# Graph diffusion by the powers S, S^2 and S^3, and the pivots of the eigenvectors written out row by row

## The chip, the cores and the metric

The kernel runs on one core of one Trainium2 chip. The metric is the device time of one execution, in microseconds (us), as the median of several runs. TensorE multiplies matrices, VectorE and ScalarE work elementwise, and each engine runs its own stream of instructions; they meet only through semaphores.

## The reference, cut to what matters

x is 16 batches of 512 nodes by 128 features, adj is 512 x 512. Four graph layers follow each other, each with a residual sum and a layer norm. The change touches the second, a diffusion of eight Euler steps:

```python
h = jnp.einsum('bnd,ed->bne', x, fc_in_w) + fc_in_b
alph = jax.nn.sigmoid(alpha_train)[:, None]
w_eff = w * jnp.clip(d, 0.0, 1.0) @ w.T
def euler_step(h, _):
    ax = jnp.einsum('nm,bmd->bnd', adj_mx, h)
    f = alph * 0.5 * (ax - h) + h @ w_eff - h + x0
    return (h + dt * f, None)
h, _ = jax.lax.scan(euler_step, h, None, length=8)
```

The third layer needs the eigenvectors U of the normalized Laplacian of adj: `_, U = jnp.linalg.eigh(L_norm)`.

## The kernel before

`build` calls one block after another: Laplacian, tridiagonal form, eigenvalues (by sweeps of the characteristic polynomials), the first layer (`graph_conv`, `lstms`), a layer norm, `turn_x`, `diffusion_terms`, and then the block that is changed, `vectors_and_diffusion`. `back_transform` and the last two layers follow. Between blocks all engines wait for each other.

`diffusion_terms` has turned the eight steps into a polynomial. The result is the sum over i from 0 to 8 of S^i x M_i plus a bias, where S (`k.S`, 512 x 512) holds adj, alpha and the step, M_i (`k.M`, nine of 128 x 128) holds the weights, and r_i (`k.r`, nine rows) the biases. `k.h` holds x turned (features on partitions), `k.x` holds x itself.

In `vectors_and_diffusion` three engines work side by side.

TensorE and ScalarE evaluate the polynomial by Horner's rule. First the bias, in nine rounds of four groups of 128 columns: lines 999 and 1002, each round after ScalarE's copies of the round before (line 1050). Then two halves of eight batches. In a half, for i from 8 down to 0, there are eight groups (two times four batches, by four blocks `nt` of 128 nodes), each in one PSUM bank of 512 columns. A group is four products of `acc` with S (line 1016, 512 columns each; none for i = 8), in the last step one with the identity that adds the bias (line 1020), and four products, one a batch, of turned x with M_i (line 1023, 128 columns each). ScalarE copies each bank to the other half of `acc`, and at last to `k.x` (line 1044). The steps from 6 to 1 stand in a loop of the engines (`Fori`).

VectorE meanwhile finds the eigenvectors of the tridiagonal matrix from its eigenvalues. It runs pivots from both ends (`way` 0 and 1): for each of 511 rows two reciprocals (line 1086) and two multiply-adds (line 1088), 128 x 4 elements each. The helper `Link` with `lag=1` lets an instruction wait for the last but one. The loop has seven rows in its body, with the row's addresses in registers, and ends with a flush and a clear of the semaphore. Then come reciprocals, scans and the squared norms (lines 1098 to 1131). ScalarE takes the root of the norms (line 1060) at a fixed place in its own order, ahead of the last but one round of copies of the second half, and VectorE goes on (line 1134 and after) to fix signs and scale `k.vec`.

The next block, `back_transform`, begins with transposes (line 1232) and needs `k.vec` and all three engines to have finished.

## Time and profile before

| | us |
|---|---|
| median of 3 runs | 5985.85 (5984.94 to 5997.67) |
| the profiled execution | 5985.78 |
| its span | 5984.1 |
| TensorE busy with matmuls | 3705.1 (62% of the span) |
| VectorE busy | 4382.6 (73%) |
| ScalarE busy | 1216.2 (20%) |
| mean granted clock of TensorE | 0.648 of 2.4 GHz |

The span runs from the first to the last instruction. Shares of the whole say little here, because the blocks have different limits: what counts for the change is the stretch from 4642 to 5322 us, in which `vectors_and_diffusion` runs. Idle time of an engine that doesn't set the end of its block costs nothing. A matmul's duration in a row includes a part in which the next one already runs, so a rate has to be read from starts.

### The profile page before, as it was taken

Reading aid. Unit: us, or ns where it says so; the run is one execution under the profiler, and the core shown is the slowest. Engines: PE = TensorE matmul, PEld = TensorE weight load, DVE = VectorE, ACT = ScalarE, POOL = GpSimd, SP = SyncE. Lnnn points to the kernel's source line nnn. Section 1 sums busy time; section 2 is a strip of 40 time slices with the busy share of each in tenths; the row PEclk is TensorE's granted clock in tenths of the full one; section 3 lists DMA queues with packets and bytes.
Section 4 is the critical chain, followed back from the end, with each engine's and each line's share of the span. In section 5 each row is a group of like instructions: output and inputs, shape, how many; then the busy total and the mean of one; then the engine's idle time right before and its main releaser. Section 6 shows DMA issues by size and latency. Waiting matters only on the chain. (4 is left out here: it accounts for less than half of the span.)

```text
span 5984.1 us, 79152 instructions
## 1 busy us (share of the span) xinstructions
PE 3705.1 (62%) x22240; PEld 2430.9 (41%) x22240; DVE 4382.6 (73%) x24246; ACT 1216.2 (20%) x3608; POOL 16.8 (0%) x30
## 2 busy tenths in 40 slices
PE   5666655555555666532333333497894999986674
PEld 4565655555555565500000000142432755553352
DVE  7888988888888877799999999612225777534457
ACT  1222122221222222221222222114321111101000
POOL 0000000000000000000000000000000000000000
PEclk9755555555555555555555555698896699988876
DMA  1000000000000000000000000000000000000001
GB/s 36 2 2 2 2 1 1 1 1 1 1 1 1 1 1 1 1 0 0 0 0 0 0 0 0 22 0 0 0 0 0 1 0 0 0 0 0 0 0 28
DMA packets 14086, 17.02 MB, mean 3 GB/s; under 512 B 624, under 2 KB 10000, under 8 KB 13712
## 3 DMA queue, kind: packets, MB, share of 16 engines
q1 hardware_dynamic: 10896, 9.44, 0.6%
q8 instruction: 157, 2.57, 0.2%
q10 hardware_dynamic: 2352, 2.69, 0.2%
q14 instruction: 217, 1.78, 0.1%
q0 software_dynamic: 464, 0.55, 0.0%
HBM read 8.47 MB, written 4.19 MB: 2 GB/s over the span
## 5 line engine op out<-in xcount | busy, mean ns | idle before, releaser
L805 DVE SCALAR_TENSOR_TENSOR poly<-poly,off,term 128x60 f32<-128x60 f32 x2560 | 608.2, 273 | 0.0
L797 DVE SCALAR_TENSOR_TENSOR term<-cut,rows,poly 128x60 f32<-128x60 f32 x2560 | 596.6, 274 | 11.2 <-DVE poly L816 2.0
L728 PE MATMUL both_signs<-signs,identb 128*128 128x480 bf16 x320 | 186.3, 582 | 569.8 <-PEq L65 569.8
L567 PE MATMUL totals<-pp_sum,ones 128*128 128x2 f32 x768 | 225.3, 363 | 410.6 <-DVE pp_sum L401 410.6
L1016 PE MATMUL horner_ps<-horner,S 128*128 128x512 f32 x1024 | 460.6, 592 | 0.0
L517 PE MATMUL row_e<-vwv 128*128 128x2 f32 (+30 forms) x988 | 301.8, 396 | 217.3 <-DVE x_parts L426 217.3
L528 PEld LDWEIGHTS product<-x_parts,A_parts 128*128 128x128 bf16 x11136 | 405.4, 111 | 42.6 <-DVE A_parts L339 42.6
L528 PE MATMUL product<-x_parts,A_parts 128*128 128x3 bf16 x11136 | 359.9, 167 | 41.6 <-DVE A_parts L339 41.6
L567 PEld LDWEIGHTS totals<-pp_sum,ones 128*128 128x128 f32 x768 | 192.3, 311 | 449.6 <-DVE pp_sum L401 449.6
L1536 PE MATMUL gate_ps<-h_sb,wih_t 128*128 x504 | 317.1, 789 | 81.7 <-PEq L65 81.7
L517 PEld LDWEIGHTS row_e<-vwv 128*128 128x128 f32 x988 | 258.6, 322 | 231.4 <-issue 231.4
L728 PEld LDWEIGHTS both_signs<-signs,identb 128*128 128x128 bf16 x320 | 40.5, 127 | 739.3 <-issue 739.3
L705 ACT ACTIVATE signs<-poly 128x1080 bf16<-128x1080 f32 x160 | 176.5, 1103 | 636.9 <-ACTq L65 636.9
L734 PE MATMUL total<-agree,identb 128*128 128x480 bf16 x320 | 153.4, 583 | 237.4 <-PEq L65 237.4
L618 ACT ACTIVATE vwv<-v,sc 128x8 f32<-128x8 f32 (+3 forms) x510 | 152.3, 299 | 652.5 <-DVE sc L384 627.3
L503 PE MATMUL change<-vwv 128*128 128x2 f32 x764 | 195.3, 348 | 117.9 <-DVE sc L432 117.4
L1016 PEld LDWEIGHTS horner_ps<-horner,S 128*128 128x128 f32 x1024 | 184.8, 190 | 183.6 <-issue 183.6
L1088 DVE SCALAR_TENSOR_TENSOR piv<-rec,sq,piv 128x4 f32 x1022 | 205.7, 223 | 64.9 <-DVE rec L1086 0.4
L512 PE MATMUL coef<-x_on_pairs_sum,ones 128*128 128x2 f32 (+30 forms) x744 | 233.5, 405 | 26.6 <-DVE x_on_pairs_sum L457 20.9
L503 PEld LDWEIGHTS change<-vwv 128*128 128x128 f32 x764 | 182.9, 319 | 133.2 <-issue 132.5
L709 ACT ACTIVATE agree<-both_signs 128x960 bf16<-128x960 f32 x160 | 155.4, 971 | 338.6 <-ACTq L65 338.6
L1536 PEld LDWEIGHTS gate_ps<-h_sb,wih_t 128*128 128x128 f32 x504 | 112.2, 227 | 265.6 <-issue 263.1
(483 smaller groups left out, 7933.1 us busy)
## 6 DMA issues: line engine op xcount, KB each, us to landing
out_dram<-x_sb SPq DMA_DIRECT2D x4, 1024.0 KB, 7.3
adj_sb<-adj_dram SPq DMA_DIRECT2D x1, 1024.0 KB, 6.0
alpha<-L_gnn_alpha_train_dram POOLq DMA_DIRECT2D x1, 256.0 KB, 5.7
edge_row<-L_gnn_src_dram POOLq DMA_DIRECT2D x1, 128.0 KB, 5.5
edge_row<-L_gnn_dst_dram POOLq DMA_DIRECT2D x1, 128.0 KB, 6.0
w<-L_gnn_Wg_dram ACTq DMA_DIRECT2D x2, 64.0 KB, 4.3
w<-L_gnn_W_dram ACTq DMA_DIRECT2D x2, 64.0 KB, 3.8
x_sb<-x_dram SPq DMA_DIRECT2D x4, 0.5 KB, 10.4
```

What stands on the lines that cost most here:

```text
L503: last = pe.matmul(norm_of(n), vwv[:, c, j % 2, 1:2].broadcast_to([P, P]), vwv[:, c, j % 2, 1:3], start=(c == c0), stop=(c == C - 1))
L512: pe.matmul(coef[:, 0:2 * j], k.ones[:], on_pairs_sum[:, 0:2 * j], start=True, stop=True)\
L517: pe.matmul(row_e[:, 0:2 * j].rearrange("p (j t) -> p j t", t=2), vwv[:, c, j % 2, 2:3].broadcast_to([P, P]), vwv[:, c, 2:2 + j, 1:3], sta ...
L528: last = pe.matmul(product[:, r, 0:PARTS], parts[:, i, c, r * P:(r + 1) * P], x_parts[:, c, :], start=(c == c0 and i == 0), stop=(c == C - ...
L567: pe.matmul(totals[:, 0:2], k.ones[:], pp_sum[:], start=True, stop=True).then_inc(dot_ready, 1)
L705: act.activation(sign[:, b], poly[:, b, :, 1:BLOCK + 2, :], ACT.Sign).then_inc(sign_full, 1)
L728: pe.matmul(here, identb[:], rows_of(b, way, 0), start=True, stop=False)
L797: pair(dve.scalar_tensor_tensor(out=term[:, way, :], in0=flat, scalar=rows[:, way, row:row + 1], in1=poly[:, b, way, s + 1, :], op0=ALU.su ...
L805: pair(dve.scalar_tensor_tensor(out=poly[:, b, way, s + 2, :], in0=poly[:, b, way, s, :], scalar=off2[:, way, row:row + 1], in1=term[:, wa ...
L1016: pe.matmul(here, k.S[:, c, nt * P:(nt + 1) * P], acc[:, src, c, j // C * 4:j // C * 4 + 4, :].rearrange("p b d -> p (b d)"), start=(c == ...
L1088: pair(dve.scalar_tensor_tensor(out=pivots(way, 1), in0=rec[:, way, :], scalar=sq[:, ds(i * per + (j + 1), 1), way], in1=pivots(way, 1), o ...
L1536: last = pe.matmul(bank[:, slot, g, 0:n].rearrange("p (b w) -> p b w", w=nw), k.wih_t[:, w + g, :], windows(s, nb, nw, i, slot, t), start= ...
```

## The change

The polynomial is evaluated by Horner's rule in S^3: with g = 2, 1, 0, the sum over g of S^(3g) (x M_3g + S x M_3g+1 + S^2 x M_3g+2).

- S is transposed (`turn`), and S^2 and S^3 are made by products (`square`, `cube`). S^2 lies in `k.u_t`.
- For every batch turned x is multiplied by S and by S^2 (`once`, `twice`) into `moved`.
- A group then takes twelve small products with M (four batches by three) and, for g = 1 and 0, four with S^3. Four batches are done at a time (q = 0 to 3), with g = 2, 1, 0 in turn. Intermediate values lie in `k.x` and `acc`.
- The bias takes three terms in place of nine rounds, with the row sums of S and S^2 (`sum`) for the powers.
- The order of all groups is the list `ORDER`, which is written out for TensorE and ScalarE; banks are taken in turn, group n in bank n % 8. `needed` and two waits inside a group say which copies must be done. ScalarE takes the root ahead of its copy of group (3, 1, 0).
- On VectorE the 511 rows of pivots are written out with fixed addresses, without the loop, its flushes and its clears. `sq` moves into the storage of `k.vec`.

The diff, without most of the removed lines:

```diff
@@ -958,14 +958,17 @@
 
     with ExitStack() as ctx:
         sb, ps, sem = allocators(nc, ctx)
-        acc = sb("horner", [P, 2, C, 8, D])
+        S2, S3 = k.u_t, sb("S3", [P, C, N])
+        moved = sb("moved_x", [P, 2, 4, N])
+        acc = sb("horner", [P, C, 4, D])
+        S_rows = acc[:].rearrange("p c b d -> p c (b d)")
         bias = sb("horner_bias", [P, 2, C, D])
+        sums = sb("sums_of_rows", [1, 2, N])
         bank = ps("horner_ps", [P, 8, N])
         full = sem("horner_full")
         free = sem("horner_free")
-        bias_used = sem("horner_bias_used")
         piv = sb("piv", [P, N, 2, C])
-        sq = sb("sq", [P, N, 2])
+        sq = k.vec[:, 0:2, :].rearrange("p c (n t) -> p (c n) t", t=2)
...
+        ORDER = [("turn", c) for c in range(C)] + [("once", b) for b in range(4)]
+        ORDER += [("square", c) for c in range(C)] + [("twice", b) for b in range(4)]
+        ORDER += [("cube", c) for c in range(C)] + [("sum", j) for j in range(2)] + [("bias", g) for g in (2, 1)]
+        for q in range(B // 4):
+            if q:
+                ORDER += [(power, q * 4 + b) for b in range(4) for power in ("once", "twice")]
+            for g in (2, 1, 0):
+                ORDER += [(q, g, nt) for nt in range(C)]
+                if (q, g) == (0, 2):
+                    ORDER.append(("bias", 0))
+        place = {step: n for n, step in enumerate(ORDER)}
+
+        def needed(step):
+
+            kind = step[0]
+            if kind == "square":
+                return place["turn", C - 1]
+            if kind == "twice" or step == ("sum", 1):
+                return place["square", C - 1]
+            if kind == "cube":
+                return place["square", C - 1]
+            if kind == "bias":
+                return place[("sum", 1) if step[1] == 2 else ("bias", step[1] + 1)]
+            if kind in range(B // 4):
+                return max(place["once", kind * 4 + 3], place["twice", kind * 4 + 3])
+            return -1
+
+        def held(q, g, c):
+
+            return acc[:, c, :, :] if g == 1 else k.x[:, c, q * 4:q * 4 + 4, :]
+
+        def turned(b, j):
+
+            return moved[:, j - 1, b % 4, :] if j else k.h[:, b, :]
...
+            for n, step in enumerate(ORDER):
+                kind, i = step[0], step[1]
+                here = bank[:, n % 8, :]
+                first = max(n - 7, needed(step) + 1)
+                if first > 0:
+                    pe.wait_ge(free, first)
+                if kind == "turn":
+                    for c in range(C):
+                        last = pe.transpose(here[:, c * P:(c + 1) * P], k.S[:, c, i * P:(i + 1) * P], k.ident[:])
+                elif kind in ("square", "cube"):
+                    right = k.S if kind == "square" else S2
+                    for c in range(C):
+                        last = pe.matmul(here, S_rows[:, c, i * P:(i + 1) * P], right[:, c, :], start=(c == 0),
+                                         stop=(c == C - 1))
+                elif kind in ("once", "twice"):
+                    by = k.S if kind == "once" else S2
+                    for c in range(C):
+                        last = pe.matmul(here, k.x[:, c, i, :], by[:, c, :], start=(c == 0), stop=(c == C - 1))
+                elif kind == "sum":
+                    by = S2 if i else k.S
+                    for c in range(C):
+                        last = pe.matmul(here[0:1, :], k.ones[:, 0:1], by[:, c, :], start=(c == 0), stop=(c == C - 1))
+                elif kind == "bias":
+                    for nt in range(C):
+                        there = here[:, nt * D:(nt + 1) * D]
+                        for j in range(3):
+                            left = sums[0:1, j - 1, nt * P:(nt + 1) * P] if j else k.ones[0:1, :]
+                            last = pe.matmul(there, left, k.r[:, 3 * i + j, :], start=(j == 0), stop=(j == 2 and i == 2))
+                        if i < 2:
+                            for c in range(C):
+                                last = pe.matmul(there, S3[:, c, nt * P:(nt + 1) * P], bias[:, (i + 1) % 2, c, :],
+                                                 start=False, stop=(c == C - 1))
+                else:
+                    q, g, nt = step
+
+                    def ahead(c):
+                        return pe.matmul(here, S3[:, c, nt * P:(nt + 1) * P],
+                                         held(q, g + 1, c).rearrange("p b d -> p (b d)"), start=(c == 0),
+                                         stop=(c == C - 1 and g == 1))
+
+                    if g < 2:
+                        pe.wait_ge(free, max(first, place[q, g + 1, 0] + 1))
+                        ahead(0)
                     for b in range(4):
-                        last = pe.matmul(here[:, b * D:(b + 1) * D], k.h[:, g * 4 + b, nt * P:(nt + 1) * P],
-                                         k.M[:, ds(i, 1), :].rearrange("p i d -> p (i d)"),
-                                         start=(src is None), stop=(src is None or b == 3))
-                    last.then_inc(full, 1)
-
-            for half in range(2):
-                step(half, STEPS, None)
-                step(half, STEPS - 1, 0)
-                with pe.Fori(0, (STEPS - 2) // 2) as n:
-                    step(half, n * -2 + (STEPS - 2), 1)
-                    step(half, n * -2 + (STEPS - 3), 0)
-                step(half, 0, 1, last_step=True)
+                        for j in range(3):
+                            last = pe.matmul(here[:, b * D:(b + 1) * D], turned(q * 4 + b, j)[:, nt * P:(nt + 1) * P],
+                                             k.M[:, 3 * g + j, :], start=(j == 0 and g == 2), stop=(j == 2 and g == 2))
+                    if g < 2:
+                        pe.wait_ge(free, max(place[q, g + 1, C - 1], place["bias", 0]) + 1)
+                        for c in range(1, C):
+                            last = ahead(c)
+                    if g == 0:
+                        last = pe.matmul(here.rearrange("p (b d) -> p b d", d=D), k.ident[:],
+                                         bias[:, 0, nt:nt + 1, :].broadcast_to([P, 4, D]), start=False, stop=True)
+                last.then_inc(full, 1)
...
+            for n, step in enumerate(ORDER):
+                kind, i = step[0], step[1]
+                here = bank[:, n % 8, :]
+                if step == (B // 4 - 1, 1, 0):
                     act.wait_ge(norm_ready, 1)
                     act.activation(root[:], norm[:], ACT.Sqrt).then_inc(root_ready, 1)
-                    evacuate(half, 1)
-                evacuate(half, None)
+                act.wait_ge(full, n + 1)
+                if kind == "turn":
+                    to = S_rows[:, i, :]
+                elif kind in ("square", "cube"):
+                    to = (S2 if kind == "square" else S3)[:, i, :]
+                elif kind in ("once", "twice"):
+                    to = turned(i, 1 if kind == "once" else 2)
+                elif kind == "sum":
+                    to, here = sums[:, i, :], here[0:1, :]
+                elif kind == "bias":
+                    to = bias[:, i % 2, :, :].rearrange("p c d -> p (c d)")
+                else:
+                    q, g, nt = step
+                    to, here = held(q, g, nt), here.rearrange("p (b d) -> p b d", d=D)
+                act.copy(to, here).then_inc(free, 1)
 
         @block.vector
         def _(dve):
@@ -1067,7 +1111,7 @@
             link(dve.tensor_tensor(k.work[:, 0:N], k.off[:], k.off[:], ALU.mult))
 
             link(dve.tensor_scalar(k.work[:, 0:N], k.work[:, 0:N], 1e-36, -1.0, ALU.max, ALU.mult))
-            link(dve.memset(sq[:], 0.0))
+            link(dve.memset(sq, 0.0))
             link(dve.tensor_copy(sq[:, 1:N, 0], k.work[:, 0:N - 1]))
             link(dve.tensor_copy(sq[:, 1:N, 1], k.work[:, 0:N - 1][:, ::-1]))
             lam_all = k.lam[:].unsqueeze(1).broadcast_to([P, N, C])
@@ -1075,21 +1119,16 @@
             link(dve.tensor_tensor(piv[:, :, 1, :], k.diag[:, ::-1].unsqueeze(2).broadcast_to([P, N, C]), lam_all,
                                    ALU.subtract))
             link.restart()
-            per = 7
             pair = Link(dve, dve_link, lag=1)
-            with dve.Fori(0, (N - 1) // per) as i:
-                for j in range(per):
-                    def pivots(way, shift):
-                        return piv[:, ds(i * per + (j + shift), 1), way, :].rearrange("p o g -> p (o g)")
-
-                    for way in range(2):
-                        pair(dve.reciprocal(rec[:, way, :], pivots(way, 0)))
-                    for way in range(2):
-                        pair(dve.scalar_tensor_tensor(out=pivots(way, 1), in0=rec[:, way, :],
-                                                      scalar=sq[:, ds(i * per + (j + 1), 1), way], in1=pivots(way, 1),
-                                                      op0=ALU.mult, op1=ALU.add))
-                pair.flush()
-                pair.restart()
+            for row in range(N - 1):
+                for way in range(2):
+                    pair(dve.reciprocal(rec[:, way, :], piv[:, row, way, :]))
+                for way in range(2):
+                    pair(dve.scalar_tensor_tensor(out=piv[:, row + 1, way, :], in0=rec[:, way, :],
+                                                  scalar=sq[:, row + 1, way:way + 1], in1=piv[:, row + 1, way, :],
+                                                  op0=ALU.mult, op1=ALU.add))
+            pair.flush()
+            link.restart()
             top = piv[:, :, 0, :].rearrange("p k g -> p g k")
             bottom = piv[:, ::-1, 1, :].rearrange("p k g -> p g k")
             diag = k.diag[:].unsqueeze(1).broadcast_to([P, C, N])
```

## Rows read from the trace of the kernel before

**Rows 1.** Busy time by stretches: length, busy us (records) of each engine, clock, DMA share, GB/s.

```profile
4642.00:4737.00 95.00, 89.98 (x330) 75.07 (x331) 71.29 (x414) 9.58 (x36) 0.00 (x0) 0.50 0.00 1
...
5087.00:5200.00 113.00, 113.00 (x419) 63.02 (x418) 79.70 (x39) 15.24 (x26) 0.38 (x1) 1.00 0.00 0
5200.00:5322.00 122.00, 120.98 (x445) 67.02 (x443) 25.19 (x138) 17.31 (x29) 0.27 (x1) 1.00 0.00 0
```

**Rows 2.** Order of time, end of the stage: start, us, engine, line, operation, operands, count [idle before].

```profile
5319.68 1.05 PE L1023 MATMUL horner_ps<-M,h_sb 128*128 128x128 f32 x8
...
5320.85 0.59 ACT L1044 COPY x_sb<-horner_ps 128x512 f32<-128x512 f32 x1 [4.60 <-ACTq L65]
...
5321.75 1.94 PE L1232 MATMUL area<-ident,neg 128*128 128x128 f32 x16 [1.02 <-PEq L959]
5321.76 1.38 DVE L1282 TENSOR_TENSOR bjunk<-tau,ident 128x128 f32<-128x128 f32 x4 [45.20 <-PEq L959]
```

**Rows 3.** Groups by line, 4640 to 5325 us: count | busy, mean ns | idle before.

```profile
L1016 PE MATMUL horner_ps<-horner,S 128*128 128x512 f32 x1024 | 460.6, 592 | 0.0
...
L1023 PE MATMUL horner_ps<-M,h_sb 128*128 (+1 forms) x1152 | 151.5, 277 | 0.7 <-PEq L65 0.7
```

**Rows 4.** Order of time, TensorE, one group of the last step.

```profile
5310.20 3.60 PE L1016 MATMUL horner_ps<-horner,S 128*128 128x512 f32 x8
...
5314.49 1.05 PE L1023 MATMUL horner_ps<-M,h_sb 128*128 128x128 f32 x8
...
5315.38 3.60 PE L1016 MATMUL horner_ps<-horner,S 128*128 128x512 f32 x8
```

**Rows 5.** Order of time, TensorE, end of the bias rounds.

```profile
4733.15 0.79 PE L999 MATMUL horner_ps<-r,ones 1*128 1x128 f32 x2
4733.88 2.08 PE L1002 MATMUL horner_ps<-horner_bias,S 128*128 128x128 f32 x8
4736.64 9.40 PE L1023 MATMUL horner_ps<-M,h_sb 128*128 128x128 f32 x64 [0.69 <-PEq L65]
```

**Rows 6.** Stretches of 6 us, TensorE alone: length, busy us, granted clock, DMA.

```profile
4740.00:4746.00 6.00, 6.00 (x51) 0.93 0.00 0
```

**Rows 7.** Order of time, VectorE: first pivots, one row of the loop, what follows.

```profile
4650.33 0.31 DVE L1086 RECIPROCAL rec<-piv 128x4 f32 x2 [0.34 <-DVE piv L1075]
...
5073.03 0.40 DVE L1088 SCALAR_TENSOR_TENSOR piv<-rec,sq,piv 128x4 f32 x2
5073.35 0.29 DVE L1086 RECIPROCAL rec<-piv 128x4 f32 x2
5073.77 0.40 DVE L1088 SCALAR_TENSOR_TENSOR piv<-rec,sq,piv 128x4 f32 x2
...
5086.48 3.98 DVE L1098 TENSOR_TENSOR adj_sb<-piv 128x2048 f32<-128x2048 f32 x1 [0.36 <-DVE piv L1088]
```

**Rows 8.** Order of time, VectorE: after the norms, after the root, the end.

```profile
5167.88 0.14 DVE L1132 COPY one<-lam 128x1 f32<-128x1 f32 x1
5246.90 0.18 DVE L1134 RECIPROCAL norm<-vroot 128x4 f32<-128x4 f32 x1 [78.88 <-ACT vroot L1060]
...
5274.50 2.05 DVE L1191 TENSOR_SCALAR neg<-neg,s 128x512 f32<-128x512 f32 x4
```

**Rows 9.** Order of time, VectorE in the last eigenvalue sweep, written out, lag 1.

```profile
3703.26 0.46 DVE L805 SCALAR_TENSOR_TENSOR poly<-poly,off,term 128x60 f32<-128x60 f32 x2
3703.64 0.46 DVE L797 SCALAR_TENSOR_TENSOR term<-cut,rows,poly 128x60 f32<-128x60 f32 x2
```

**Rows 10.** Order of time, VectorE in `join`, written out, each waits for the last.

```profile
5248.67 0.23 DVE L1149 TENSOR_SCALAR s<-s,one 128x4 f32<-128x4 f32 x1
5248.93 0.16 DVE L1150 TENSOR_TENSOR s<-s 128x4 f32<-128x4 f32 x1
```

**Rows 11.** Order of time, VectorE in the tridiagonal block, written out, independent instructions.

```profile
1000.49 0.23 DVE L438 SCALAR_TENSOR_TENSOR vwv<-vt_half,sc,side 128x3 f32<-128x3 f32 x1
1000.63 0.23 DVE L426 SCALAR_TENSOR_TENSOR x_parts<-x_scaled,totals,y_scaled 128x3 bf16<-128x3 f32 x1
```

More of the change, by code:

```diff
@@ L988, in _ @@
+        def held(q, g, c):
+            return acc[:, c, :, :] if g == 1 else k.x[:, c, q * 4:q * 4 + 4, :]
+        def turned(b, j):
+            return moved[:, j - 1, b % 4, :] if j else k.h[:, b, :]
         @block.tensor
         def _(pe):
-            def rows_of(half, j):
-                return half * 2 + j // C, j % C
-            for i in range(STEPS, -1, -1):
-                if i < STEPS:
-                    take(pe, bias_used, C)
-                for nt in range(C):
-                    here = bank[:, nt, 0:D]
-                    last = pe.matmul(here, k.ones[0:1, :], k.r[:, i, :], start=True, stop=(i == STEPS))
-                    if i < STEPS:
-                        for c in range(C):
-                            last = pe.matmul(here, k.S[:, c, nt * P:(nt + 1) * P], bias[:, (i + 1) % 2, c, :],
-                                             start=False, stop=(c == C - 1))
-                    last.then_inc(full, 1)
@@ L1005, in _ @@
-            take(pe, bias_used, C)
-            def step(half, i, src, last_step=False):
-                for j in range(8):
-                    g, nt = rows_of(half, j)
-                    if nt == 0:
-                        take(pe, free, C)
-                    here = bank[:, j, :]
-                    if src is not None:
-                        for c in range(C):
-                            pe.matmul(here, k.S[:, c, nt * P:(nt + 1) * P],
-                                      acc[:, src, c, j // C * 4:j // C * 4 + 4, :].rearrange("p b d -> p (b d)"),
-                                      start=(c == 0), stop=False)
-                    if last_step:
-                        pe.matmul(here.rearrange("p (b d) -> p b d", d=D), k.ident[:],
-                                  bias[:, 0, nt:nt + 1, :].broadcast_to([P, 4, D]), start=False, stop=False)
-                    for b in range(4):
-                        last = pe.matmul(here[:, b * D:(b + 1) * D], k.h[:, g * 4 + b, nt * P:(nt + 1) * P],
-                                         k.M[:, ds(i, 1), :].rearrange("p i d -> p (i d)"),
-                                         start=(src is None), stop=(src is None or b == 3))
-                    last.then_inc(full, 1)
@@ L1036, in _ @@
         @block.scalar
         def _(act):
-            def evacuate(half, to):
-                for j in range(8):
-                    g, nt = half * 2 + j // C, j % C
-                    take(act, full)
-                    there = k.x[:, nt, g * 4:g * 4 + 4, :] if to is None else acc[:, to, nt, j // C * 4:j // C * 4 + 4, :]
-                    act.copy(there, bank[:, j, :].rearrange("p (b d) -> p b d", d=D)).then_inc(free, 1)
-            act.nop().then_inc(free, 2 * C)
-            for i in range(STEPS, -1, -1):
-                for nt in range(C):
-                    take(act, full)
-                    act.copy(bias[:, i % 2, nt, :], bank[:, nt, 0:D]).then_inc(bias_used, 1)
@@ L1051, in _ @@
-            for half in range(2):
-                evacuate(half, 0)
-                evacuate(half, 1)
-                with act.Fori(0, (STEPS - 2) // 2 - half) as _:
-                    evacuate(half, 0)
-                    evacuate(half, 1)
-                if half:
-                    evacuate(half, 0)
+            for n, step in enumerate(ORDER):
+                kind, i = step[0], step[1]
+                here = bank[:, n % 8, :]
+                if step == (B // 4 - 1, 1, 0):
                     act.wait_ge(norm_ready, 1)
@@ L1060, in _ @@
                     act.activation(root[:], norm[:], ACT.Sqrt).then_inc(root_ready, 1)
-                    evacuate(half, 1)
-                evacuate(half, None)
+                act.wait_ge(full, n + 1)
[12 more added lines that the diff above has]
+                    to, here = held(q, g, nt), here.rearrange("p (b d) -> p b d", d=D)
```

## Prediction

> **What bounds the kernel now.** The change touches one stage, the block `vectors_and_diffusion`, so I read that stage and not the whole span. First the busy time by stretches [rows 1]: from 4642 us to 5322 us TensorE is busy in nearly all of each stretch (the three rows shown stand for six), while VectorE has 71 of 95 us at the beginning and 25 of 122 us at the end. The granted clock is 0.50 in the first 95 us, that is 1.2 GHz, and 1.00 (2.4 GHz) in the last stretches. Then the end of the stage [rows 2]: the last product ends at 5320.7, ScalarE's last copy out of PSUM follows, and the next block starts on TensorE and VectorE together at 5321.8; VectorE had stood idle for 45 us before that. So TensorE sets the end of this stage, and the stage lasts 5321.7 - 4642.1 = 679.6 us. What comes after it starts 0.9 us after the last product and isn't touched.
>
> VectorE is second. It works through the pivots from 4650.33 to 5086.1 [rows 7], reaches `norm` at 5168.0, waits 78.9 us for ScalarE's root, because ScalarE takes the root only at its place among the copies, and then has 29.6 us to go (5246.9 to 5276.5) [rows 8]. If TensorE gets much shorter, this second chain can become the bound; the sum has to be made for both.
>
> **Rates of TensorE.** In the trace a product of fp32 operands is two records: the code has 512 products with S of 512 columns and 576 products with M of 128, the trace shows 1024 and 1152 [rows 3]. At the full clock, from one group with S to the next is 5315.38 - 5310.20 = 5.18 us [rows 4]. In it are four products with S, one with the identity (512 columns each) and four with M; those with M take 5315.38 - 5314.49 = 0.89 us, so a small product costs 0.223 us and a large one (5.18 - 0.89) / 5 = 0.858 us. As a trial on the stage before: 512 x 0.858 + 576 x 0.223 + 16 x 0.858 = 581 us against 584 us between 4736.64 and 5320.7. The rates hold.
>
> A small product is as cheap by the column as a large one. The page "TensorE: Matmul & The Clock Gate" of the Trainium skill (section "Back-to-back issue gap") speaks against a change to many small products: it gives about 81 ns for each matmul of 128 columns that has its own weight load. Here 0.223 us is four such passes, 56 ns each [rows 4], so the trace disagrees with 81. By the page's figure, as an estimate, 644 small products would cost 4 x 25 ns more each, 65 us in all, and the sum would be 5801 us; I go by the row.
>
> **The change on TensorE.** The Horner loop with S falls away, and so do the nine bias rounds at 1.2 GHz (94 us, 4642.1 to 4736.6). In their place, all at the full clock but where said:
> - turn S: 16 transposes. The same count in the next block takes 1.94 us [rows 2]; 2.0 us.
> - x by S for four batches, 16 large products, 13.7 us. They start cold. In the trace the dense run began at 4736.64 [rows 5] and the stretch from 4740 on already has 0.93 [rows 6]; with the transposes ahead of them I allow 7 us at half the clock, which loses 3.5 us.
> - S^2, x by S^2, S^3: 3 x 16 large products, 41.2 us. The two row sums: 8 products, 6.9 us.
> - three bias terms: 36 small products with one-row weights and 32 with S^3, 68 x 0.223 = 15.2 us. Bounds: nothing more, or the old bias price. There a one-row product and four with S took 0.73 + 2.08 us at 1.2 GHz [rows 5]. By these rows the two terms that stand alone (24 one-row products and 16 with S^3) would cost 24 x 0.73 + 16 x 0.52 = 25.8 us in place of 8.9, 17 us more. I take 6 us of them, a third, because the old rounds started cold and these follow 80 us of dense work.
> - x by S and S^2 for the other twelve batches: 96 x 0.858 = 82.4 us.
> - the main part: 4 x 3 x 4 groups of 12 small products, 576 x 0.223 = 128.4 us; 32 groups with four products by S^3, 109.8 us; 16 with the bias by the identity, 13.7 us.
> - new waits. `needed` makes a product wait for the copy just before it in six places (S^2 before "twice", the sum before bias 2, bias 2 before bias 1, and "twice" before the first group of q = 1, 2, 3). In the old trace TensorE stood from 4735.96 to 4736.64 around a copy of 0.27 us [rows 5]; with a copy of 0.59 us [rows 2] that is 1.0 us each, 6 us. The other waits are for copies that end while TensorE has 2.7 us or more of other products. ScalarE has about 100 copies of 0.59 us, some 60 us in all, and doesn't bound.
>
> Sum: 2.0 + 13.7 + 3.5 + 41.2 + 6.9 + 15.2 + 6 + 82.4 + 128.4 + 109.8 + 13.7 + 6 = 428.8 us. From 4642.1 the last product ends at 5070.9, the next block begins at 5071.8 in place of 5321.75. That is 249.9 us less.
>
> **The change on VectorE.** Four instructions a row as before, 511 rows. Now the body takes 0.74 us a row (5073.03 to 5073.77), and over all (5086.1 - 4650.33) / 511 = 0.853 us, for every seventh row ends in a loop edge [rows 7]. Written out, the edge goes. What the body becomes is not in the loop's rows, since in the loop the addresses come from registers. From the second reciprocal (5073.35 + 0.12) to the next multiply (5073.77) are 0.30 us, though the first reciprocal's result is ready at 5073.53: that gap isn't the data's. Upper bound: 0.742 us, only the edges go. Lower bound: from the nearest written-out code. In the eigenvalue sweep, with the same pairing, pairs follow each other at 0.38 us with no gap, at 60 elements [rows 9], so a stream of such instructions isn't held up. A written-out instruction that needs the last one's result starts 0.03 us after its end (5248.67 + 0.23, then 5248.93) [rows 10], and one of this kind that needs nothing starts 0.14 us after the one ahead of it [rows 11]. So a row is reciprocal 0.18 + 0.03, multiply, 0.14 to the second multiply, 0.14 to the next reciprocal: 0.49 us. I take 0.49, because it is built of rows of written-out code. The pivots then take 251 us in place of 436, and `norm` is ready at 5168 - 185 = 4983.
>
> **Where the two meet.** ScalarE takes the root ahead of its copy of group (3, 1, 0). TensorE then has g = 1 and g = 0 still to do, 4 x (2.7 + 3.4) + 4 x (2.7 + 3.4 + 0.86) = 52 us, so ScalarE stands there at about 5020. `norm` at 4983 is 37 us early. VectorE gets the root at about 5020 and ends some 31 us later, at 5051, 20 us ahead of TensorE. So the pivots pay nothing by themselves; they have to be under about 0.6 us a row, or else ScalarE, and behind it every bank, waits for `norm`. `sq` lying in `k.vec` costs nothing, since the scans write there only after the last pivot. The profiled execution took 5985.78 us, 1.68 us over its span, and the median of the runs is 5985.85, so I count from either: 5985.8 - 249.9 = 5735.9, say 5736.
>
> **Rivals.**
> - The pivots keep the loop's 0.742 us (or something over 0.6). For it: no row shows this very body written out. Against it: [rows 9 to 11]. `norm` comes at 5168 - 57 = 5111. TensorE finishes g = 1 at about 5043 and stands idle. After 5111 come the root 1.5, a copy 0.6, four groups of 6.96 us, some 3.5 us for the clock, which fell in the idle time, and the last copy: the next block begins at about 5147, that is 5811 us. The change would then not do what its second half says.
> - TensorE loses some tens of us more: the clock falls in the bias terms and stays low into the first groups, or the six waits are longer. For it: the cold bias rounds of [rows 5]. Each 20 us at 1.2 GHz costs 10. 5750 to 5775.
> - Slower than before: the mix of one-row products, small products and short waits keeps TensorE at 1.2 GHz, as it did for 95 us with 90 us busy [rows 1]. The place is the whole stage, 413 us of products. All of it at half the clock is 5736 + 400 = 6136 us; it is slower than before from about 250 us at half the clock on. Against it: before, the clock was 0.93 within the first 9 us of small products with M, and all that followed, a fifth of it small products, ran at 1.00 [rows 1, 6].
>
> **How the numbers follow.** Forecast (5724 to 5750) 0.78; TensorE some tens slower 0.12; pivots not under 0.6 us a row 0.07; slower than before 0.02; within 0.2% 0.01. 0.2% is about what a measurement of this kernel can tell from no change. The low end, 5724, is no cold bias (-6), no ramp (-3.5) and half the waits (-3); the high end, 5775, takes in the second rival and leaves out 1 in 10. Faster 0.97, same 0.01, slower 0.02.
>
> **What would show it.** The stage should go from 4642 to about 5072, with the granted clock at 1.00 from about 4650 on, perhaps broken at the bias terms. The pivots' pairs should start 0.49 us a row apart and end near 4902; VectorE should wait for the root about 35 us and stand idle some 20 us at the end. A row of 0.6 us or more, a copy of ScalarE's held by `norm`, or small products above 0.223 us at the full clock would make the prediction wrong.

## The result, and the profile after

The changed kernel takes 5750.6 us (median of 4 runs, 5748.7 to 5753.7) against 5986.7 for the kernel before (4 runs on the same chip): ratio 0.960, 95% interval 0.959 to 0.961. The prediction was 5736 us, between 5724 and 5775. Its profiled execution took 5752.2 us, with a span of 5750.4, that is 233.7 us less than the 5984.1 before.

The stage first, as in [rows 1]. Busy time by stretches of the changed kernel; columns as there (length, then TensorE, its weight loads, VectorE, ScalarE and GpSimd, then the clock, DMA share, GB/s):

```profile
4642.00:4656.00 14.00, 14.00 (x40) 7.52 (x39) 13.44 (x65) 4.08 (x7) 0.00 (x0) 0.93 0.00 1
4656.00:4740.00 84.00, 81.98 (x319) 49.32 (x318) 84.00 (x703) 12.28 (x21) 0.00 (x0) 0.92 0.00 1
4740.00:4760.00 20.00, 20.00 (x93) 15.30 (x93) 20.00 (x169) 1.17 (x2) 0.00 (x0) 0.75 0.01 2
4760.00:4900.00 140.00, 139.32 (x645) 88.42 (x644) 139.76 (x1120) 16.80 (x29) 0.00 (x0) 1.00 0.00 1
```

TensorE is still busy throughout. The 0.93 of the first stretch is its start at 1.2 GHz; from then on it runs at the full clock but for two dips, which show as 0.92 and 0.75. The end of the stage, as in [rows 2], in order of time. PE is TensorE, ACT ScalarE and DVE VectorE; square brackets hold the engine's idle time before a row and what ended it:

```profile
5072.04 2.74 PE L1064 MATMUL horner_ps<-horner,S 128*128 128x512 f32 x6
...
5074.62 1.02 PE L1080 MATMUL horner_ps<-horner_bias,ident 128*128 128x512 f32 x2
...
5075.68 0.59 ACT L1106 COPY x_sb<-horner_ps 128x512 f32<-128x512 f32 x1 [6.38 <-PE horner_ps L1080]
...
5076.57 1.39 DVE L1321 TENSOR_TENSOR bjunk<-tau,ident 128x128 f32<-128x128 f32 x4 [21.44 <-PEq L959]
```

The products still set the end, and VectorE stood idle for 21 us before it, in place of 45. The stage began at 4640.8 (4642.1 before) and lasted 435.8 us in place of 679.7: 243.9 us less. VectorE's pivots and what follows them, as in [rows 7], and at last the two lines that answer to [rows 8]:

```profile
4780.21 0.30 DVE L1125 RECIPROCAL rec<-piv 128x4 f32<-128x4 f32 x2
4780.42 0.35 DVE L1127 SCALAR_TENSOR_TENSOR piv<-rec,neg,piv 128x4 f32<-128x4 f32 x2
4780.69 0.30 DVE L1125 RECIPROCAL rec<-piv 128x4 f32<-128x4 f32 x2
...
4894.06 3.98 DVE L1137 TENSOR_TENSOR adj_sb<-piv 128x2048 f32<-128x2048 f32 x1 [0.21 <-DVE piv L1127]
...
4975.46 0.14 DVE L1171 COPY one<-lam 128x1 f32<-128x1 f32 x1
5025.47 0.18 DVE L1173 RECIPROCAL norm<-vroot 128x4 f32<-128x4 f32 x1 [49.87 <-ACT vroot L1091]
```

A row takes 0.48 us, the pivots end at 4893.9, `norm` is ready at 4975.5 and the root comes at 5025.4, on time for TensorE.

Where 233.7 us come from: 1.2 from the earlier start, 243.9 from the stage, and then 11.5 are lost behind it, in blocks that the diff doesn't touch. `back_transform`, from its first instruction on VectorE to its last copy (`u_t`), took 105.5 us before (5321.8 to 5427.3) and 113.0 after (5076.6 to 5189.6); what follows took 556.8 and 560.8. This loss was not in the prediction, and half of the experiments are about it. It is read from one profiled execution of each kernel; by the medians the gain is 236.1 us, so that some 8 us of the stage's 243.9 are lost elsewhere, about as much as the ratio's interval is wide (7 us to either side).

### The profile page after: what moved, and what is told of

The parts are those of the page before. It is cut to its first block and busy times, and to the rows that moved or that the text cites. A ratio compares the mean times of both kernels' runs of the same rounds, so it can differ in the third digit from the quotient of the medians.

```text
span 5750.4 us, 75645 instructions
## 1 busy us (share of the span) xinstructions
PE 3473.0 (60%) x21632; PEld 2307.1 (40%) x21632; DVE 4306.5 (75%) x24246; ACT 1179.1 (21%) x3525; POOL 16.8 (0%) x30
## 5 line engine op out<-in xcount | busy, mean ns | idle before, releaser
L728 PE MATMUL both_signs<-signs,identb 128*128 128x480 bf16 x320 | 186.2, 582 | 570.7 <-PEq L65 570.7
L615 ACT ACTIVATE root<-totals,tiny 128x1 f32<-128x1 f32 x256 | 66.8, 261 | 701.8 <-PE totals L500 701.8
L512 PEld LDWEIGHTS coef<-x_on_pairs_sum,ones 128*128 128x128 f32 x744 | 187.2, 312 | 41.4 <-DVE x_on_pairs_sum L457 36.1
L729 PE MATMUL both_signs<-signs,identb 128*128 128x480 bf16 x320 | 193.7, 605 | 0.0
```

Source lines behind the costliest of these rows:

```text
L512: pe.matmul(coef[:, 0:2 * j], k.ones[:], on_pairs_sum[:, 0:2 * j], start=True, stop=True)\
L728: pe.matmul(here, identb[:], rows_of(b, way, 0), start=True, stop=False)
L729: last = pe.matmul(here, identb[:], rows_of(b, way, 1), start=False, stop=True)
```

## The experiments

Several runs give a `ratio` to the kernel before on the same chip, since chips differ: it took 5991.9 to 5994.8 us beside the experiments. The last three columns are lengths from the one profiled execution of each, read from the starts: the stage, `back_transform` up to its last copy, and the rest to the end. The recorded expectations give the last two columns as one figure that is 11.9 us smaller (661.9 us for 673.8 in the changed kernel, 650.4 for 662.3 in the one before), and `back_transform` with the start of the layer norm as one that is 19.7 us larger.

Executions of one kernel on one chip spread by up to 10 us: the five of the changed kernel beside `best` lie between 5748.1 and 5758.3 us. Differences of a few us between single runs say little by their times; the length of the stage came out alike to 0.1 us where a stage was profiled twice.

| kernel | median us | ratio (interval) | stage | back_transform | rest |
|---|---|---|---|---|---|
| before | 5986.7 | | 679.7 | 105.5 | 556.8 |
| before, second profile | | | 679.7 | 104.5 | 560.8 |
| changed | 5750.6 | 0.9601 (0.9589 to 0.9613) | 435.8 | 113.0 | 560.8 |
| changed, again | 5755.5 | 0.9598 (0.9585 to 0.9611) | 435.8 | 113.0 | 560.8 |
| diff_only | 5880.8 | 0.981 (0.9793 to 0.9826) | 558.5 | 113.2 | 560.7 |
| piv_only | 5998.9 | 1.0003 (0.9994 to 1.0013) | 679.7 | 111.5 | 560.7 |
| long_body | 5847.5 (one run) | | 528.3 | 113.7 | 556.9 |
| full_height | 5744.2 | 0.9581 (0.9565 to 0.9597) | 421.8 | 113.4 | 560.7 |
| tight | 5729.8 | 0.9565 (0.9549 to 0.9581) | 416.0 | 108.8 | 561.0 |
| shift1 | 5749.7 (one run) | | 436.2 | 109.3 | 560.6 |
| shift3 | 5749.5 (one run) | | 432.6 | 109.6 | 560.6 |
| warm | 5730.3 | 0.9564 (0.9548 to 0.958) | 435.7 | 89.1 | 560.8 |
| before_warm | 5972.5 | 0.9963 (0.9949 to 0.9978) | 679.7 | 89.9 | 555.6 |
| best | 5709.4 | 0.9524 (0.9511 to 0.9537) | 416.1 | 89.1 | 557.0 |

### Which half brings the time: diff_only and piv_only

In diff_only the written-out pivots are put back into the old loop of seven rows:

```diff
-            for row in range(N - 1):
...
+            per = 7
+            with dve.Fori(0, (N - 1) // per) as i:
...
```

> The new diffusion with the old loop of pivots. My theory: the two halves of the change need each other, because ScalarE takes the root at its place among the copies. The pivots take 436 us as before and `norm` is ready at about 5167; TensorE stands idle from about 5048, the clock falls, and after 5167 come the root 1.5 us, a copy 0.6, the four groups of g = 0 (27.9), some 3.5 for the clock and the last copy: the stage ends at about 5202 in place of 5076, the time is 5877 us (5870 to 5885). Rival: the gain is TensorE's alone and the written-out pivots are an ornament: 5751 us, within 5 us of the changed kernel.

Measured: 5880.8 us, ratio 0.981. Of the changed kernel's gain about 125 us are missing, as my theory had it and not the rival. ScalarE in this kernel, and then TensorE, in order of time:

```profile
5025.03 1.28 ACT L1091 ACT_TABLE_LOAD   x1
5172.61 0.20 ACT L1091 ACTIVATE vroot<-norm 128x4 f32<-128x4 f32 x1 [146.30 <-DVE norm L1175]
5172.73 2.03 ACT L1106 COPY horner<-horner_ps 128x512 f32<-128x512 f32 x4
```

```profile
5046.11 2.74 PE L1064 MATMUL horner_ps<-x_sb,S 128*128 128x512 f32 x6
5173.44 2.05 PE L1064 MATMUL horner_ps<-horner,S 128*128 128x512 f32 x2 [124.59 <-ACT horner L1106]
```

ScalarE stands 146 us in front of the root with four finished banks behind it, and TensorE 125 us for the first of their copies. When it goes on, two records take 2.05 us where they take 1.02 warm: the clock had fallen in the idle time.

piv_only is the other half alone: the kernel before with the 511 rows written out.

> The kernel before with its pivots written out and nothing else. My theory: VectorE is off the path here, `norm` is ready at about 4976 in place of 5168 and VectorE waits some 270 us for the root in place of 79; time 5986 us, the same within the few us that the later blocks' clock may move. Rival: part of the 236 us comes from the pivots alone; then this kernel is faster than before by that part, up to 190 us (5796).

Measured: ratio 1.0003, and the wait it was expected to lengthen:

```profile
4981.05 0.14 DVE L1127 COPY one<-lam 128x1 f32<-128x1 f32 x1
5251.27 0.18 DVE L1129 RECIPROCAL norm<-vroot 128x4 f32<-128x4 f32 x1 [270.08 <-ACT vroot L1060]
```

So the diffusion alone gives 1.9%, the pivots alone nothing, both together 4.0%. The pivots are worth their 2% only behind the new diffusion, since only there VectorE would be late.

### Why a written-out row is faster: long_body

```diff
-            per = 7
+            per = 73
```

(in the loop of diff_only)

> The changed kernel with the pivots again in a loop, but with 73 rows in the body and 7 rounds in place of 7 rows and 73 rounds. Theory A: the row's 0.74 us in the loop come from the addresses in registers, so the row stays at 0.74 us here, only 66 edges of 0.8 us go, `norm` comes at about 5115, TensorE waits for it, and the time is about 5825 us. Theory B: the edges disturbed the whole body and a row falls to about 0.48 us in a long body too: 5751 to 5755 us.

Measured: the row stays at 0.74 us. So theory A holds for the body: it is the addresses in registers, not the edge, that cost 0.26 us a row. But the time was 5847.5 and not 5825, since an edge of the long body is dearer than one of the short. VectorE at the first edge:

```profile
4709.46 0.30 DVE L1130 RECIPROCAL rec<-piv 128x4 f32 x2
4709.89 0.40 DVE L1132 SCALAR_TENSOR_TENSOR piv<-rec,neg,piv 128x4 f32 x2
4713.56 0.31 DVE L1130 RECIPROCAL rec<-piv 128x4 f32 x2 [3.27 <-issue]
```

3.3 us of idle time in which the engine waits for nothing that the profile shows, where an edge of the seven-row body costs 7 x (0.853 - 0.742) = 0.8 us in all [rows 7]. The pivots lasted 4655.0 to 5061.1, 406 us: 511 x 0.742 = 379 and 27 us more, of which six edges are 20.

### What the clock fell on in the bias terms: full_height and tight

In the changed kernel TensorE's clock dips twice. Its products around the first dip, in order of time (1*128 are weights of one row, 128*128 of full height):

```profile
4709.97 0.38 PE L1055 MATMUL horner_ps<-r,ones 1*128 1x128 f32 x2
4710.19 0.60 PE L1055 MATMUL horner_ps<-r,sums_of_rows 1*128 1x128 f32 x4
4711.47 0.48 PE L1055 MATMUL horner_ps<-r,ones 1*128 1x128 f32 x2 [0.68 <-ACT horner_bias L1106]
4711.79 0.60 PE L1055 MATMUL horner_ps<-r,sums_of_rows 1*128 1x128 f32 x4
4712.33 2.08 PE L1058 MATMUL horner_ps<-horner_bias,S 128*128 128x128 f32 x8
4714.34 0.79 PE L1055 MATMUL horner_ps<-r,ones 1*128 1x128 f32 x2
```

From 4712 the same products take about twice as long (eight records 2.0 us, not 0.9). Ahead of that stood the term 2, one-row products alone, and a wait. The second dip comes in the third term, in the middle of small products at the full clock and with no wait near it:

```profile
4738.21 0.48 PE L1055 MATMUL horner_ps<-r,ones 1*128 1x128 f32 x2
4739.07 1.57 PE L1058 MATMUL horner_ps<-horner_bias,S 128*128 128x128 f32 x8
4740.57 0.79 PE L1055 MATMUL horner_ps<-r,ones 1*128 1x128 f32 x2
```

full_height replaces only the one-row products. It leaves out the bias and serves for the timing alone:

```diff
-                            left = sums[0:1, j - 1, nt * P:(nt + 1) * P] if j else k.ones[0:1, :]
-                            last = pe.matmul(there, left, k.r[:, 3 * i + j, :], ...)
+                            last = pe.matmul(there, k.ident[:], k.M[:, 3 * i + j, :], ...)
```

> The changed kernel with the 36 one-row products of the bias terms replaced by products of full height (identity by M, same columns, same count). The bias values are left wrong by this. Theory A: the one-row products are what the clock fell on at 4712 and again at 4740; with full height the clock stays at 1.00 from 4646 to 5076 and the stage is some 11 us shorter, 5740 us. Theory B: the waits and the small products with S^3 do it; then the same two stretches at 0.50 stay and the time is 5751 us.

Measured: the stage is 14.0 us shorter, and the clock doesn't fall. (The ratio is lower by 0.002, some 11 us, no more than its interval; the stage's length is the sharper measure.) Its products of the term 1, in order of time, and the whole stage as one stretch (TensorE: length, busy us, clock):

```profile
4717.31 0.94 PE L1054 MATMUL horner_ps<-M,ident 128*128 128x128 f32 x6 [0.67 <-ACT horner_bias L1105]
4718.09 1.06 PE L1057 MATMUL horner_ps<-horner_bias,S 128*128 128x128 f32 x8
4718.98 0.83 PE L1054 MATMUL horner_ps<-M,ident 128*128 128x128 f32 x6
```

```profile
4650.00:5068.00 418.00, 413.52 (x1914) 1.00 0.00 1
```

The waits are still there (0.67), the count of products is the same. What the clock fell on were the products with one row. The first dip stands in the traces of all seven profiles with one-row products in the new diffusion, and in none of the three at full height (full_height, tight, best).

tight makes a proper version of this: row r in a tile of 128 rows that is zero but for the first, the row sums by all 128 ones, and the order of `ORDER` changed so that no product waits for the copy just ahead of it.

```diff
+            link(dve.memset(k.r[:], 0.0))
...
-        ORDER += [("square", c) for c in range(C)] + [("twice", b) for b in range(4)]
+        ORDER += [("square", c) for c in range(C)] + [("sum", 0)] + [("twice", b) for b in range(4)]
+        ORDER += [("sum", 1)] + [("cube", c) for c in range(C)] + [("bias", 2)]
...
-                if (q, g) == (0, 2):
-                    ORDER.append(("bias", 0))
+                if q == 0 and g:
+                    ORDER.append(("bias", g - 1))
...
-                        last = pe.matmul(here[0:1, :], k.ones[:, 0:1], by[:, c, :], ...)
+                        last = pe.matmul(here, k.ones[:], by[:, c, :], ...)
...
+                        if g == 2 and nt == 0 and b == 3:
+                            pe.wait_ge(free, place["twice", q * 4 + 3] + 1)
...
```

> The changed kernel with the bias terms' one-row products at full height (row r in a tile that is zero in its other rows, the row sums by all 128 ones, so the result is the same), the sums and bias terms moved in between the large products so that no product waits for the copy just ahead of it, and the first group of each q waiting for its last batch alone. Theory A: the clock stays at 1.00 (11 us) and five or six waits of 0.7 us go: the stage lasts about 418 us in place of 436, the ratio to the kernel before is about 0.957. Theory B: the bias terms between other work still let the clock fall; then only the waits go and the ratio is 0.9595.

Measured: stage 416.0 us, 19.8 less than the changed kernel's, ratio 0.9565. TensorE has no idle time left between its products:

```profile
4646.00:5056.00 410.00, 410.00 (x1910) 1.00 0.00 1
```

It is 5.8 us shorter than in full_height, which has the six waits: nearly 1 us a wait, as forecast. The 0.66 to 0.68 us of idle time that stand in the rows are only part of that price, since the records overlap. Around the wait for the row sums in the changed kernel:

```profile
4703.59 3.60 PE L1049 MATMUL horner_ps<-u_t,ones 128*1 128x512 f32 x8
4707.85 0.48 PE L1055 MATMUL horner_ps<-r,ones 1*128 1x128 f32 x2 [0.66 <-ACT sums_of_rows L1106]
```

Four large products are 3.43 us, but from start to start there are 4.26, and the first small product behind the wait takes 0.33 us in place of 0.22: 0.94 us for this wait.

### Where 11.5 us went behind the stage: shift1, shift3, warm, before_warm

The 7.5 us lost in `back_transform` could be the clock's doing: there TensorE and VectorE take turns, and the clock goes up and down. TensorE in that block, before and after (the stretches are 105 us; length, busy us, clock; over the whole block of the changed kernel, 113.0 us with the same 264 records as before, the clock is 0.70):

```profile
5322.00:5427.00 105.00, 68.02 (x264) 0.79 0.00 0
```

```profile
5076.00:5181.00 105.00, 70.40 (x240) 0.67 0.00 0
```

shift1 and shift3 move the block by adding one or three copies at the end of the stage:

```diff
+            for j in range(3):
+                act.copy(moved[:, 0, j, :], bias[:, 0, :, :].rearrange("p c d -> p (c d)"))
```

> The changed kernel with one more copy (0.6 us) by ScalarE at the end of the stage, of values nobody reads. Theory A: from `back_transform` on, the time depends on where its idle times fall against the steps of the clock; so the 661.9 us from its start to the end change by some us up or down, not at all by a fixed amount, and could come to the 650 of the kernel before. Theory B: the 11 us were brought by the change in a fixed way: 662 us again, the whole 0.6 us later.

> The same with three more copies, 1.8 us. Theory A: the time from the start of `back_transform` to the end is neither that of the changed kernel (661.9 us) nor that with one copy, but another value between 645 and 665. Theory B: 662 us again.

Measured: `back_transform` 109.3 and 109.6 us in place of 113.0. So its time is not fixed: it came out 3 to 4 us shorter without any change in its work. That the start decides it is not shown. The two shifts hardly differ, though theory A wanted a third value from the second; neither comes back to 105; and by the first instruction's place in the span the order is changed kernel 5076.6 (113.0), shift3 5077.6 (109.6), shift1 5077.9 (109.3), changed kernel again 5079.7 (113.0). Their stages, with one and three copies more, should have been 0.6 and 1.8 us longer; that of shift3 is 3.2 shorter. The third bias term in it and in the changed kernel, one stretch behind the first dip's start and one in the third term for each (TensorE: length, busy us, clock), shift3 first:

```profile
4716.00:4730.00 14.00, 14.00 (x60) 0.52 0.01 2
4738.00:4752.00 14.00, 14.00 (x106) 1.00 0.01 2
```

```profile
4712.00:4724.00 12.00, 12.00 (x50) 0.51 0.01 2
4738.00:4750.00 12.00, 12.00 (x51) 0.57 0.00 1
```

So the first dip came in both and the second only in the changed kernel, with the same products. diff_only and long_body have the first dip alone, too (their clock is 1.00 from 4741 to 4757, around the third term). One-row products don't let the clock fall each time, and what decides it stays open.

warm goes at the cause itself and fills TensorE's idle times there with products that nobody reads:

```diff
-            def mine(last):
+            def mine(last, fill=1):
                 turn[0] += 1
                 last.then_inc(pe_done, 1)
+                for _ in range(fill):
+                    pe.matmul(spare[:, 0:256], k.ident[:], k.adj_t[:, 0, 0:256], start=True, stop=True)
                 pe.wait_ge(dve_done, turn[0])
...
```

The longer idle times get three or four such products.

> The changed kernel with products into a spare bank (identity by adj turned, 256 columns, one to four of them) put on TensorE in `back_transform` behind each group, where it stands waiting for VectorE. Theory A: the 7 to 8 us that `back_transform` lost against the kernel before, and more, are the clock, which goes up and down there with the short idle times; with filled idle times it stays at 1.00, the block with the layer norm's start (132.7 us in the changed kernel, 125.2 in the one before) falls to 105 to 112 us and the time by 20 to 27 us. Theory B: the loss is not the clock's but belongs to how this stage ends; then the fill gives nothing, or costs what it delays.

Measured: `back_transform` 89.1 us, 23.9 less than in the changed kernel, with the clock at 1.00. TensorE in it, one stretch, and one round in order of time:

```profile
5078.00:5171.00 93.00, 75.02 (x370) 1.00 0.00 1
```

```profile
5097.36 0.39 PE L1288 MATMUL area<-pw 128*128 128x128 f32 x2
5097.58 1.46 PE L1269 MATMUL spare<-adj_t,ident 128*128 128x256 f32 x6
5099.30 1.16 PE L1291 MATMUL area<-inv,pw 128*128 128x128 f32 x8 [0.26 <-DVEq L1320]
```

The fill ends 0.26 us ahead of the next real product, and in no round of the block is the idle time behind it shorter, so it delays nothing. In the changed kernel a pair of records of these rounds starts every 0.43 us, here every 0.22.

before_warm puts the same fill behind the old diffusion.

> The kernel before with the same fill in `back_transform` and nothing else. Theory A: with the clock held, `back_transform` lasts the same behind either diffusion (108.8 us to the layer norm's start, as behind the new one), and what lies between this kernel and the changed one with the fill is the stage alone: 244 to 248 us, or 249 to 252 if the next layer's beginning falls differently by 4 us; time about 5972 us against 5990, ratio 0.997. Theory B: behind the old diffusion the block is shorter by 7 to 11 us by nature: about 100 us.

Measured: 89.9 us for the block, against 89.1 behind the new diffusion. With the clock held, the block is as long behind either to 0.8 us, so what it had lost against the kernel before was the clock. Between warm and before_warm lie 242.6 us of span, just under the 244 to 248 forecast: 244.0 from the stage, 3.1 from where it starts, 0.8 from the block, less 5.2 in the rest. The second profile of the kernel before says what its first left open:

> The kernel before once more, for a second profile. Theory A: from the start of `back_transform` to the end it took 650.4 us in the first profile only by how the clock's steps fell; here it may take any of the values seen behind either diffusion, 650 to 662 us. Theory B: 650 us again, since this kernel keeps what the change lost.

Measured: 104.5 us for the block and 560.8 for the rest. So of the 11.5 us the 4.0 in the rest are a fall that the kernel before has too (556.8 once, 560.8 once). In `back_transform`, though, it has again 104.5, near its first value, while every kernel with the new diffusion and no fill lies between 108.8 and 113.7. piv_only, which has the old diffusion, has 111.5. So the clock is the cause, as before_warm shows. Theory B (650 us again) failed: in its count the second profile has 653.4, in theory A's range, but the difference is the rest's and not the block's. The two kernels that were profiled twice came near their own value each time (113.0 and 113.0, 105.5 and 104.5). Two profiles each are too few to say that it will always be so, and what sets the value isn't shown. The start alone is not it, by the four starts above; and piv_only, whose block begins within 1.6 us of that in before_again, behind the same last products, has 7.0 us more. Which value a change will meet stays open.

### Both improvements together: best

> Both together: the stage with full-height bias products and without the waits, and the filled idle times of `back_transform`. If the two gains (21 us of the stage and of what follows, 24 us of `back_transform`) are of different places they add up: about 20 us from the stage and 20 us from `back_transform`, where the clock's steps cost nothing any more; ratio to the kernel before about 0.953, 5707 us against 5990. If the second only gave back what the first had moved, the ratio stays at 0.956.

> The changed kernel itself beside it on the same chip, for the difference: ratio 0.960, 5750 us against 5990. By theory A of the clock, its time from the start of `back_transform` to the end may come out some us apart from the 661.9 of the first time; by theory B it is 662 again.

Measured: the changed kernel repeats its three lengths to 0.1 us, as theory B said. best takes 5709.4 us, ratio 0.9524, against 0.9598 for the changed kernel beside it: 46 us less. Stage 416.1 and block 89.1: the two gains add up, 19.7 and 23.9 us, and 3.8 of the rest came along. This version is faster than both kernels.

## Why the prediction was right, point by point

**The number.** 5750.6 us lie in the range, but at the upper edge of the part to which I gave 0.78 (5724 to 5750), by some tenths in that of the second rival (5750 to 5775). The first part of the way there is that rival's mechanism, the clock in the bias terms. The second, the time lost behind the stage, was in no term and no rival; that the range had room for it was luck.

**What bounds.** TensorE sets the end before and after: right. VectorE idle at the end for 21 us, forecast 20; `norm` is ready 48 us before ScalarE asks for it, in place of 37.

**The rates.** 0.858 and 0.223 us carry over: 32 records of `once` from 4644.19 to 4657.93 are 13.74 us (forecast 13.7), and one group of g = 0 takes 5075.68 - 5068.71 = 6.97 us (6.96). This is the rows' rate. By the 81 ns for a pair of weight load and product that stand in "TensorE: Matmul & The Clock Gate" of the Trainium skill, "Back-to-back issue gap", each small product would, as an estimate, have cost 0.1 us more, and the stage 65; the trace doesn't agree.

**The sum.** 428.8 us were forecast from the first instruction to the last product, 434.8 came (4640.84 to 5075.6). By its terms:
- turn S: 3.4 us in place of 2.0. The row that I took was a warm one [rows 2]; here the clock was still at 1.2 GHz.
- the ramp: nothing in place of 3.5. `once` ran at the full rate from its first product; the clock had risen by the end of the transposes.
- the bias terms: this is the term that was mis-sized. Forecast were 15.2 us and 6 more for the clock. The first two terms took 17.1 us (4707.85 to 4724.94, a wait inside) and the third 11.3 (4736.26 to 4747.59). In full_height they take 10.0 (4713.69 to 4723.67, with the same wait) and 6.2 (four parts of 1.56). So the clock cost 7.1 us in the first two, 5.1 in the third and, as the stage is 14.0 us longer in all, 1.8 in the products right behind them. The 6 us that I had allowed for the first two nearly fit: a third of the cold price of 17. The step that failed is that the third term was put down as warm, at nothing. "These follow 80 us of dense work" held for no more than the term 2, and 11 us at the full clock ahead of the third term didn't protect that one.
- waits: six, each near 0.94 us from start to start (0.66 to 0.68 of it shown as idle), 5.6 in place of 6.

So 8.0 us too little for the clock and 1.4 for the transposes were in part made up for by 3.5 too much for the ramp and 0.4 for the waits: 5.5 of the 6.0 us.

**Pivots.** Forecast 0.49 us a row, measured 0.479; forecast end 4902 at a start of 4650.3, that is 251 us, measured 245 from 4648.9. The model from written-out rows held, and so did the reading that the gap in the loop is not the data's: long_body keeps the row at 0.742. The price of a wrong row was right too: diff_only, with the loop and its edges, gave 5881 against 5877 written down for it.

**The rivals.** The second (the clock falls in the bias terms) came true in part, with 14.0 us in place of the 6 in the sum; the clock stayed low for no more than the first products of the groups behind. The first did not, but diff_only shows its mechanism. The slower one did not: from 4754 to 5076 the clock was 1.00 throughout.

**What was missing.** The sum took everything behind the stage as unchanged. It lost 11.5 us of span there in the profiled pair: 7.5 in `back_transform`, where the clock was lower with the same work (what decides that is open), and 4.0 further on, which the kernel before loses too in its second profile. Forecast gain 249.9, measured 233.7: 6 from the stage, 12 from behind it, less 1.2 for the earlier start, with some tenths of rounding.

## What to carry to other kernels

When two engines share a block, look for the instruction where one waits for the other at a fixed place in its own order: shortening one engine is paid only up to the point at which that wait turns, and the change that moves the other engine (worth nothing by itself, 1.0003) can be worth half of the whole (0.981 to 0.960). Price a loop's row by what stands between its instructions; here the operands were long ready, the addresses in registers were the price, and writing the rows out removed it. And where a block alternates between engines with idle times of one to three microseconds, don't take its time as fixed: with the same work it took 104.5 to 113.7 us, and filling the idle times with products gave 24 us at the price of one spare bank.

## What the runs showed of the hardware

- One-row products at the full rate let TensorE's clock fall to 1.2 GHz in the middle of dense work, twice in the changed kernel (once in shift3, diff_only and long_body), and cost 14.0 us; the same columns with 128 rows held it at 1.00 for the whole stage.
- 16 transposes of 128 columns, started at 1.2 GHz after 6.7 us of idle time, were followed by products at 2.4 GHz from their start (4644.19).
- A loop edge on VectorE cost 0.8 us with seven rows in the body and 3.3 us with 73. "Runtime: NRT & Kernel Launch" of the Trainium skill, "Instruction fetch mechanics", says that a taken branch to code outside the current pages has to fetch it before going on; the 3.27 us that the trace puts down to issue agree with that, though no row shows the fetch itself.
- Four instructions of VectorE with fixed addresses take 0.48 us, with addresses from registers 0.74.
